# Token scatters of a graph layer in one row after the last gather, with transfers split to even row counts

## What is computed

```python
xn = layernorm(x)
# graph part: mean of xn over the incoming edges of each node
neigh = segment_sum(xn[src], dst) / max(deg, 1)
h = layernorm(xn @ W_self.T + neigh @ W_neigh.T + bias) * gamma + beta
# attention part: phi = elu + 1, one context matrix for all nodes
a = (phi(q) @ (phi(k).T @ v)) / (phi(q) @ sum(phi(k)))
x = x + h + a @ w_out.T + b_out
# expert part
t = layernorm(x)
p = softmax(t @ gate_w.T + gate_b); top2 = top_k(p, 2)
x = x + sum_shared(gelu(t @ sw1.T + sb1) @ sw2.T + sb2) \
      + sum_top2(p_e * (gelu(t @ rw1_e.T + rb1_e) @ rw2_e.T + rb2_e))
```

## Time and profile before

| | us |
|---|---|
| median of 3 runs | 2593.32 |
| lowest, highest run | 2586.42, 2600.19 |
| profiled execution | 2580.17 |
| its span | 2578.2 |
| TensorE busy | 2118.4 (82%) |
| VectorE busy | 1754.7 (68%) |
| GpSimd busy | 1397.2 (54%) |
| ScalarE busy | 707.3 (27%) |

### The profile page before, as it was taken

How to read it: one execution, slowest core, us unless ns; L and a number is a source line. 1 busy time by engine, 2 the same in 40 slices (tenths; PEclk the granted TensorE clock), 3 DMA queues, 4 the chain that set the end, 5 groups by cost and what they waited for, 6 DMA issues and landing times.

```text
span 2578.2 us, 44862 instructions
## 1 busy us (share of the span) xinstructions
PE 2118.4 (82%) x13129; PEld 1458.1 (57%) x13130; DVE 1754.7 (68%) x3522; ACT 707.3 (27%) x1264; POOL 1397.2 (54%) x1416
## 2 busy tenths in 40 slices
PE   0089999668888888898888887988449999979999
PEld 0057777445556555565555555655336666657776
DVE  5667777457888878788787887888524444436666
ACT  0434444111222122111221122211214444423332
POOL 0034444477777777777777777776122222224443
PEclk9999999889999999899999998999769999999999
DMA  7343433367778887888889787887454454457776
GB/s 272 111 153 138 140 134 137 111 189 240 231 192 240 219 230 209 188 245 222 225 198 227 223 233 203 213 229 191 80 152 160 162 164 163 163 163 248 258 244 210
DMA packets 179988, 496.99 MB, mean 193 GB/s; under 512 B 43284, under 2 KB 48404, under 8 KB 178667
## 3 DMA queue, kind: packets, MB, share of 16 engines
q0 software_dynamic: 96960, 314.93, 43.5%
q1 hardware_dynamic: 67516, 137.81, 18.2%
q10 hardware_dynamic: 15471, 43.74, 4.3%
HBM read 373.81 MB, written 122.45 MB: 192 GB/s over the span
## 4 chain that ended last, share of the span: by engine, by line
PE 43%; DVE 19%; DMA 13%; issue 10%; POOL 4%; ACT 3%; DVEq 1%; SPq 1%; PEld 0%; POOLq 0%; PEldq 0%; ACTq 0%
PE bank L291 8%; PE bank L292 8%; PE bank L293 8%; PE bank L936 4%; DMA region<-table,idx 4%; DVE region L1519 3%; DMA ebuf<-edges 2%; DMA region<-table,ebuf 2%; PE bank L890 2%; DMA Wff<-table,ebuf 2%; DVE Wff L1379 2%; PE bank L1071 2%; PE bank L1124 2%; PE bank L1126 2%; PE bank L1125 2%
## 5 line engine op out<-in xcount | busy, mean ns | idle before, releaser
L597 POOL DMA_INDIRECT region<-table,idx x122 | 115.3, 945 | 316.9 <-PE bank L1071 266.6
L544 POOL DMA_INDIRECT region<-table,ebuf x225 | 223.8, 995 | 77.7 <-issue 68.2
L544 POOL DMA_INDIRECT Wff<-table,ebuf x225 | 228.5, 1016 | 68.4 <-issue 67.5
L551 POOL DMA_INDIRECT Wff<-table,ebuf x200 | 224.5, 1123 | 60.9 <-issue 60.9
L936 PE MATMUL bank<-Wff 128*125 128x512 f16 x850 | 206.4, 403 | 39.1 <-DMA Wff<-table,ebuf 39.1
L551 POOL DMA_INDIRECT region<-table,ebuf x200 | 200.0, 1000 | 60.9 <-issue 52.7
L936 PE MATMUL bank<-region,ohs 128*125 128x512 f16 x850 | 205.5, 403 | 30.9 <-DMA region<-table,ebuf 30.9
L734 ACT ACTIVATE region<-bank,sv 128x500 f32<-128x500 f32 x50 | 33.7, 674 | 663.7 <-DVE region L1503 663.7
L562 POOL DMA_INDIRECT slots<-tok,posi x100 | 149.8, 1498 | 95.6 <-DVE before L1493 65.7
L291 PE MATMUL bank<-Wsn,region 128*125 128x512 f16 x400 | 166.1, 415 | 35.3 <-ACT region L734 35.3
L936 PEld LDWEIGHTS bank<-Wff 128*125 128x125 f16 x850 | 120.2, 145 | 115.0 <-DMA Wff<-table,ebuf 44.6
(11 more groups left out here) (275 smaller groups left out, 5600.1 us busy)
## 6 DMA issues: line engine op xcount, KB each, us to landing
yd<-region ACTq DMA_DIRECT2D x59, 512.0 KB, 3.0
x2d<-region SPq DMA_DIRECT2D x25, 512.0 KB, 11.0
region<-x2d SPq DMA_DIRECT2D x25, 512.0 KB, 5.1
region<-x SPq DMA_DIRECT2D x50, 250.0 KB
table<-region POOLq DMA_DIRECT2D x50, 250.0 KB, 6.2
xnt<-region POOLq DMA_DIRECT2D x25, 500.0 KB, 2.9
region<-xnt SPq DMA_DIRECT2D x25, 500.0 KB, 5.3
region<-x SPq DMA_DIRECT2D x25, 500.0 KB
```

The lines of the kernel that those rows point to most:

```text
L544: pool.indirect_dma_start(out=ring[j][:, s, :], out_offset=None, in_=table, in_offset=bass.IndirectOffsetOnAxis(ap=ebuf[j][:, 2 * s:2 * s ...
L551: pool.indirect_dma_start(out=ring[j][:, s, :], out_offset=None, in_=table, in_offset=bass.IndirectOffsetOnAxis(ap=ebuf[j][:, 2 * s:2 * s ...
L597: pool.indirect_dma_start(out=tg[:, c, :], out_offset=None, in_=table2, in_offset=bass.IndirectOffsetOnAxis(ap=idx[:, 2 * turn + c:2 * tur ...
```

## The change

The scatters leave the loop: after the last gather, `dispatch(i)` is called for all 25 groups, 100 scatters in a row. They now read `pos` itself, which holds the positions of all tiles, and `tok` becomes a table of all 50 tiles, filled once by an iota with a pitch of 128 per tile. So `table2` gets 128 rows per tile, 6400 in all, and its store writes all 128 partitions. `posi`, its wait and the addition to `tok` go; the gate has 17 steps a group instead of 19. Since the scatters read `pos` later, its overwriting with the shifted positions moves behind the third stage and waits for all scatters. The loads of x are split into 112 and 13 rows, in both stages that load it.

```diff
-    table2 = nc.dram_tensor("table2", [N, 2 * D], F16).ap()
+    table2 = nc.dram_tensor("table2", [NT * 128, 2 * D], F16).ap()
...
-        posi = sb("posi", [T, 2, 2], I32)
-        tok = sb("tok", [T, 2], I32)
+        tok = sb("tok", [T, NT], I32)
...
-        tab2 = carve(region2, 2 * G * D, F16, T).rearrange("p (j n) -> p j n", j=G)
+        tab2_all = carve(region2, 2 * G * D, F16).rearrange("p (j n) -> p j n", j=G)
+        tab2 = tab2_all[0:T]
...
-                    sp.dma_start(xa[j], x[bass.ds(i * GT + j * T, T), :]).then_inc(pair("x_in")[j], 16)
+                    sp.dma_start(xa[j][0:T16], x[bass.ds(i * GT + j * T, T16), :]).then_inc(pair("x_in")[j], 16)
+                    sp.dma_start(xa[j][T16:T], x[bass.ds(i * GT + j * T + T16, T - T16), :]).then_inc(pair("x_in")[j], 16)
...
-                sp.dma_start(xg, x[bass.ds(i * GT, GT), :].rearrange("(j p) n -> p j n", j=G)).then_inc(sem["xg_in"], 16)
+                rows = x[bass.ds(i * GT, GT), :].rearrange("(j p) n -> p j n", j=G)
+                sp.dma_start(xg[0:T16], rows[0:T16]).then_inc(sem["xg_in"], 16)
+                sp.dma_start(xg[T16:T], rows[T16:T]).then_inc(sem["xg_in"], 16)
...
-                sp.dma_start(table2[bass.ds(i * GT, GT), :].rearrange("(j p) n -> p j n", j=G), tab2).then_inc(sem["rows2_out"], 16)
+                sp.dma_start(table2[bass.ds(i * G * 128, G * 128), :].rearrange("(j p) n -> p j n", j=G), tab2_all).then_inc(sem["rows2_out"], 16)
...
-            pool.iota(tok[:], [[T, 2]], base=-GT, channel_multiplier=1).then_inc(sem["ident_set"], 1)
+            pool.iota(tok[:], [[128, NT]], base=0, channel_multiplier=1).then_inc(sem["ident_set"], 1)
...
             def dispatch(i):
-                placed_in = of(pool, GATE_STEPS * i + 17)
-                pool.wait_ge(sem["consts"], 1)
-                pool.wait_ge(sem["gate_dve"], placed_in)
+                pool.wait_ge(sem["gate_dve"], GATE_STEPS * i + 15)
                 for j in range(G):
                     for k in range(2):
                         pool.indirect_dma_start(
-                            out=slots, out_offset=bass.IndirectOffsetOnAxis(ap=posi[:, j, k:k + 1].bitcast(U32), axis=0),
-                            in_=tok[:, j:j + 1], in_offset=None,
+                            out=slots, out_offset=bass.IndirectOffsetOnAxis(ap=pos[:, G * i + j, k:k + 1].bitcast(U32), axis=0),
+                            in_=tok[:, G * i + j:G * i + j + 1], in_offset=None,
                         ).then_inc(sem["scat"], 16)
...
                 gathers(i + 1, 0)
-                dispatch(i - 2)
                 gathers(i + 1, 1)
-            dispatch(NG - 3)
-            dispatch(NG - 2)
-            dispatch(NG - 1)
+            for i in range(NG):
+                dispatch(i)
...
-                if past(i):
-                    dve.wait_ge(sem["scat"], 64 * i)
-                dve.tensor_copy(posi[:], posf[:]).then_inc(done, 1)
                 dve.tensor_copy(pos[:, bass.ds(2 * i, 2), :], posf[:]).then_inc(done, 1)
-                ts(tok[:], tok[:], GT, None, ALU.add).then_inc(done, 1)
...
-            dve.tensor_copy(pos[:].rearrange("p t k -> p (t k)"), P2).then_inc(sem["pos_set"], 1)
             dve.tensor_copy(sched2[:, 0:NE + 1], a[:, 0:NE + 1]).then_inc(sem["sched2_set"], 1)
...
             made(NE - 1, hi)
 
 
+            dve.wait_ge(sem["scat"], 64 * NG)
+            dve.tensor_copy(pos[:].rearrange("p t k -> p (t k)"), P2).then_inc(sem["pos_set"], 1)
```

More of the change, by code:

```diff
@@ L202, in gps_layer_kernel @@
         res = [carve(region1, G * D).rearrange("p (j n) -> p j n", j=G) for _ in range(2)]
-        region2 = sb("region2", [128, 11168], F32)
+        region2 = sb("region2", [128, 11152], F32)
         at[0] = 0
@@ L1244, in statistics @@
                 for j in range(G):
-                    dve.wait_ge(pair("x_in")[j], 16 * (i + 1))
+                    dve.wait_ge(pair("x_in")[j], 32 * (i + 1))
                     dve.bn_stats(st[:, j, :], src[j]).then_inc(sem["ln_step"], 1)
@@ L1426, in _ @@
             dve.memset(x2_all[96:128], 0.0).then_inc(sem["x2_pad"], 1)
-            dve.wait_ge(sem["x2_pad"], 1)
+            dve.memset(tab2_all[96:128], 0.0).then_inc(sem["x2_pad"], 1)
+            dve.wait_ge(sem["x2_pad"], 2)
             def means(g, j):
@@ L1485, in places @@
                 dve.wait_ge(done, base + 14)
-                if past(i):
-                    dve.wait_ge(sem["scat"], 64 * i)
-                dve.tensor_copy(posi[:], posf[:]).then_inc(done, 1)
                 dve.tensor_copy(pos[:, bass.ds(2 * i, 2), :], posf[:]).then_inc(done, 1)
-                ts(tok[:], tok[:], GT, None, ALU.add).then_inc(done, 1)
                 tt(before[:], before[:], chosen[:, 0, :], ALU.add).then_inc(done, 1)
-                dve.wait_ge(done, base + 18)
+                dve.wait_ge(done, base + 16)
                 tt(before[:], before[:], chosen[:, 1, :], ALU.add).then_inc(done, 1)
-                assert GATE_STEPS == 19
+                assert GATE_STEPS == 17
             def group(i, prev, nxt):
@@ L1531, in group @@
                     onehots(nxt, 1)
-                dve.wait_ge(sem["xg_in"], 16 * (i + 1))
+                dve.wait_ge(sem["xg_in"], 32 * (i + 1))
                 tt(xg, xg, beta_bc[0:T, None, :].broadcast_to([T, G, D]), ALU.add).then_inc(sem["h_gam"], 1)
@@ L1679, in _ @@
             combine(NG - 1, 0)
-GATE_STEPS = 19
+GATE_STEPS = 17
 NORM_STEPS = 6 + 3 * NEWTON
```

## The result

The kernel after takes 2616.94 us (median of 4 runs, 2616.25 to 2627.92) beside 2589.91 us of the kernel before in the same series: a ratio of 1.0108, 95% interval 1.0067 to 1.0149. It is slower, by 27 us, where I had forecast 128. The profiled execution has a span of 2615.4 us, 37.2 more than before. 33.8 of these are there when the third stage makes its first transpose (1934.53 against 1900.68), 3.4 come later.

What follows compares the result with a forecast made beforehand. GpSimd was taken to bound the middle stage's loop, TensorE the first stage. A shorter loop, then a 290 us row of scatters, starts the third stage 128 us later: 2580 + 128 = 2708, given as 2720 us; range 2590 to 2785.

Steps and rivals of the forecast that it cites:

- The bound of the loop: Middle stage's loop: GpSimd's indirect DMAs hold it at 52.2 us a pass, while TensorE alone would need about 50.
- its new length: Middle stage's loop without scatters: a pass of 49.9 us (48.5 to 50.4), saving 48 us by group 22's store of x2.
- The row's price: 100 scatters after the last gather: memory paces them at 2.9 us each, 290 us, the last landing at 2020 us.
- The upper bound: Price of one scatter in the row: 5.6 us, from the dispatch beside the reload of weights.
- rival 1: Row of scatters: GpSimd sets its pace, landing at 1882 us, third stage at 1891, 2583 us in all; chance 0.12.
- rival 2: Row of scatters: single DMA engines set the cost, 1.6 to 2.4 us each, 2591 to 2671 us in all; chance 0.20.
- The turning point: Row of scatters: it hides if a scatter costs the memory under 1.6 us.
- The start of the third stage: Third stage's first transpose: 9 us after the last scatter lands, at 2029 instead of 1900.7 us.
- The rest: Position copy at the third stage's end, iota and memsets at the start, split x loads, 128-row table2 stores: nothing.
- The 12 us that I added: Whole kernel: step from the profiled execution's 2708 us to the 2720 given for the median.

Runs made afterwards that it cites:

- f1: Kernel before with split loads of x and 128-row stores of table2 (the balanced transfers) alone, scatters staying in the loop: 2566.79 us against 2584.11, ratio 0.9923.

## Why the prediction was wrong, point by point

**The bound of the loop (right), its new length (off).** GpSimd held the loop: with four scatters of 125 rows in it the pass is 52.2 us, balanced or not, without them 51.06, and GpSimd has time to spare. I took 2.3 us a pass from the pass, by giving back all of TensorE's wait for gathered rows; it was 1.2. The wait went, but that for VectorE's places grew from 24.2 to 38.9 us in 1000. The store of x2 of group 22 came at 1707 and not at 1696, the last gather at 1739.4 and not at 1730: 10 us too early. Of the 37 us gained at that store, 12 were gained before the loop's steady part, and f1 shows that they belong to the balanced transfers, which I had put at nothing. My reason was that TensorE is busy throughout the first stage. That holds from 200 us on; at its start it waits for x through VectorE, and the split loads bring that start forward by 8 us.

**The row's price (wrong; this is the step that failed).** The term was 100 x 2.9 = 290 us, with the memory as what paces the row. It measured 185 us from the first issue to the last landing, of which 146.5 at GpSimd's pace. The 2.9 came from one dispatch of four, 11.6 us from its first packet to the end of its effects, divided by four. But a single scatter takes 8.9 us to land with nothing beside it; four of them 1.48 us apart take 4.4 + 8.9 = 13.3 us from the first issue to the last landing, and scatters alone keep the DMA engines busy for 0.07 of the time. I read a latency as a rate. The upper bound, 5.6 us, was made the same way. This one term accounts for the miss: it was 105 us too long, the row began 11 us later than forecast, and the third stage starts 94 us before my 2029.

**What speaks for rival 1 and rival 2.** Rival 1, GpSimd's pace, is the mechanism of most of the row, down to "the slow packets are the price of mixing". It lacked the pauses: without them the last scatter would have landed at about 1901. It is not 1882, because the row also began 11 us later and the last scatter needs 8.9 us to land, where I had 2. Rival 2's band, 1.6 to 2.4 us each, holds the 1.85 us, and its 2591 to 2671 us hold the 2617. That is luck: its reason, single DMA engines that pace the row, isn't what the runs show. Scatters alone leave these engines busy for 0.07 of the time, and the 1.85 us are GpSimd's 1.48 and the pauses, longer instructions and last landing spread over 100. That 128 rows changed GpSimd's price and the pauses speaks for some part of the spread over engines, which the traces don't show.

**The turning point (right).** I had it at 1.6 us a scatter. With the row's true start it would have been (1891.8 - 1739.4) / 100 = 1.52. With everything in it the row of after costs 1.85 us each, and the third stage starts later than before; with 128 rows it is (1881.0 - 1739.3) / 100 = 1.42 us, and the third stage starts 11 us earlier than before. It isn't hidden even so: it starts 92 us behind the last x2 store, against 60 with the scatters in the loop.

**The start of the third stage (right).** 8.6 us after the landing (1925.9 to 1934.5), I had 9. **The rest (right behind that start, where only 3 us changed; wrong at the first stage, as said above).** The 12 us that I added to come from the profiled execution to the median were not there: the profiled execution of the kernel after, 2617.03 us, is its median.

The range, 2590 to 2785, holds 2616.9, by way of rival 2; the forecast's own 2671 to 2771 doesn't. The chance of slower by more than 0.5% was 0.77, and slower it is. The direction came out by a narrower margin than the sum had: 1.85 us against a turning point of 1.5 to 1.6, of which 0.25 us are pauses that I hadn't foreseen.

## What to carry to other kernels

The time from the first issue to the last effect of a short batch is mostly latency; a price for a long row needs a second length, or a stretch where the engines' share shows who is waiting. Work taken off the engine that bounds a loop pays only down to the next bound (here 1.2 us a pass for 7.4 us of scatters), while at the end of the stage it counts in full as soon as its cover is used up (here after some 50 of 100). In the row, 128 rows instead of 125 brought the third stage's start 45 us forward (1934.5 to 1889.5), nearly as much as putting the scatters of 125 rows back into the loop (48 us, f1); in the loop their gain isn't shown (0.9892 against 0.9923, with intervals that overlap). And a term put at nothing because an engine is busy throughout a stage should be checked at the stage's start too: the split loads of x gained 8 us there.

## What the runs showed of the hardware

- An indirect DMA with 125 rows costs GpSimd 1.18 us and one with 128 rows 0.97 us, each with 0.30 us behind it. I had expected three rows more to cost a little more.
- In a row of 125-row scatters GpSimd pauses before the 40th and the 79th, in all nine runs with so long a row, for 7 to 20 us at the first and, in the six that had all 100, for 5 to 13 us at the second. With 128 rows there is no pause in 100. It looks as if something fills after 39 of them; that wasn't tested.
- Scatters alone keep the DMA engines busy for 0.07 of the time, but what runs beside them falls from 425 to 111 GB/s at a share of 0.99. 128 rows don't heal that (154 GB/s from 1820 to 1870 us, 146 in the kernel after).
- Splitting the first stage's loads of 125 rows into 112 and 13 halves VectorE's wait for them at the stage's start (31.1 to 15.6 us).
- Some of GpSimd's indirect DMAs take 1.9 to 3 us instead of 1 (2.71 us at 1743.68 above). In the row of the kernel after this happens only while VectorE works; after 1825, when VectorE is idle, it doesn't. The Trainium skill, DMA: Bandwidth & Descriptors, SWDGE vs HWDGE vs iDMA, says that VectorE locks GpSimd out of the memory in which it writes its descriptors while it runs in its 2-port mode; the trace agrees in so far as it happens only beside VectorE's work, and shows neither mode nor cause.
